# Decoder layer on one core: a second V buffer, five output places, and a table of places for each group of a batch

## What is computed

```python
x = x + _L0_attn_ref(_layernorm(x), wq, bq, wk, bk, wv, bv, wo, bo)   # q, k, v, softmax(q k^T) v, wo
x = x + _L0_xattn_ref(_layernorm(x), ctx_512, Wq, Wkv_expand, Wout)   # keys and values from the latent, causal
x = x + _L0_ffn_ref(_layernorm(x), proj1, proj1_bias, proj2, proj2_bias, gate_w)  # gelu(x p1 + b1) p2 + b2
```

## Time and profile before

| | us |
|---|---|
| median of 3 runs | 1224.34 (1221.7 to 1225.97) |
| the profiled execution | 1223.58 |
| its span, first to last instruction | 1221.8 |
| TensorE busy | 1162.2 (95%) |
| VectorE busy | 674.4 (55%) |
| ScalarE busy | 483.3 (40%) |
| GpSimd busy | 431.5 (35%) |

### The profile page before, as it was taken

The page is one execution under the profiler, slowest core; times in us unless marked ns, Lnnn a source line. Parts: engine busy times, 40 slices in busy tenths (PEclk is TensorE's granted clock), DMA queues, the critical chain, the costliest instruction groups (busy, mean ns, idle before and its releaser), DMA issues.

```text
span 1221.8 us, 15866 instructions
## 1 busy us (share of the span) xinstructions
PE 1162.2 (95%) x6016; PEld 774.1 (63%) x6016; DVE 674.4 (55%) x966; ACT 483.3 (40%) x792; POOL 431.5 (35%) x398
## 2 busy tenths in 40 slices
PE   5989999999999899999999999999999999999998
PEld 4645566466556544555656565655787887887886
DVE  5656757665776467567667567564454233233222
ACT  4345544545453556535445454554131111111110
POOL 1226632643444756534426347564101001001000
PEclk9979999999999999999999999999999999999999
DMA  6823322342143434514525436420320000000000
GB/s 234 265 87 116 110 77 74 107 122 86 55 119 104 138 109 125 151 62 141 164 86 150 118 104 190 122 69 1 95 87 1 35 1 1 34 0 0 35 1 35
DMA packets 73735, 110.30 MB, mean 90 GB/s; under 512 B 6976, under 2 KB 45888, under 8 KB 71744
## 3 DMA queue, kind: packets, MB, share of 16 engines
q1 hardware_dynamic: 70864, 102.00, 27.8%
q0 software_dynamic: 2080, 6.82, 2.0%
q10 hardware_dynamic: 720, 0.54, 0.1%
HBM read 71.58 MB, written 37.75 MB: 89 GB/s over the span
## 4 chain that ended last, share of the span: by engine, by line
PE 83%; DVE 8%; POOL 3%; ACT 3%; issue 2%; DMA 1%; SPq 0%; DVEq 0%; ACTq 0%; POOLq 0%
PE PS L865 17%; PE PS L866 16%; PE PS L867 16%; PE PS L997 12%; PE PS L982 9%; PE PS L960 8%; DVE m_cols L1203 5%; PE PS L992 2%; PE PS L985 1%; PE PS L963 1%; DVE xTL L1169 1%; ACT PT L784 1%; POOL P_sum L648 1%; POOL P_sum L654 1%; PE PS L879 1%
## 5 line engine op out<-in xcount | busy, mean ns | idle before, releaser
L1203 DVE TENSOR_REDUCE m_cols<-PS 128x1 f32<-128x512 f32 (+3 forms) x432 | 281.8, 668 | 170.2 <-PE PS L960 96.8
L784 ACT ACTIVATE PT<-PS 128x512 f32<-128x512 f32 (+1 forms) x432 | 240.4, 580 | 158.0 <-PE PS L982 69.0
L648 POOL TENSOR_TENSOR P_sum<-PT 128x512 f32<-128x512 f32 x128 | 161.4, 1281 | 355.0 <-ACT PT L784 354.9
L960 PE MATMUL PS<-stackK,stackQ 96*128 96x512 f32 (+3 forms) x512 | 188.3, 404 | 12.2 <-DVE m_cols L1203 10.3
L982 PE MATMUL PS<-stackQ,stackK 100*128 100x512 f32 (+3 forms) x512 | 181.9, 399 | 6.7 <-ACT PT L784 6.5
L837 ACT ACTIVATE hid<-PS,b1c 128x512 f32<-128x512 f32 x64 | 44.1, 690 | 280.2 <-PE PS L867 278.2
L1284 DVE CAST hidH<-hid 128x512 fp32r<-128x512 f32 x64 | 30.6, 478 | 225.0 <-ACT hid L837 222.9
L960 PEld LDWEIGHTS PS<-stackK,stackQ 96*128 96x128 f32 x512 | 92.4, 192 | 80.8 <-DVE m_cols L1203 45.0
L1211 DVE RECIPROCAL P_sum<-PS 128x512 f32<-128x512 f32 x32 | 107.5, 3358 | 56.3 <-PE PS L997 56.3
L982 PEld LDWEIGHTS PS<-stackQ,stackK 100*128 100x128 f32 x512 | 90.3, 190 | 67.5 <-ACT PT L784 30.3
L654 POOL TENSOR_TENSOR P_sum<-P_sum,PT 128x512 f32<-128x512 f32 x96 | 120.5, 1282 | 4.5
(11 more groups left out here) (112 smaller groups left out, 1685.9 us busy)
## 6 DMA issues: line engine op xcount, KB each, us to landing
scratch<-stage SPq DMA_DIRECT2D x128, 256.0 KB, 2.9
stackK<-scratch SPq DMA_DIRECT2D x62, 256.0 KB, 3.9
stackQ<-scratch SPq DMA_DIRECT2D x46, 256.0 KB, 3.7
stackQ<-scratch SPq DMA_DIRECT2D x18, 512.0 KB, 4.8
stackK<-scratch SPq DMA_DIRECT2D x60, 128.0 KB, 4.1
stackQ<-scratch SPq DMA_DIRECT2D x28, 128.0 KB, 3.6
PT<-wT SPq DMA_DIRECT2D x3, 1024.0 KB, 8.6
x_res<-x SPq DMA_DIRECT2D x3, 1024.0 KB, 9.1
```

What stands on the lines that cost most here:

```text
L648: pool.tensor_tensor(P_sum[:, h, :], PT[:, h, :], PT[:, 4 + h, :], ALU.add).then_inc(p_added, 1)
L784: nc.scalar.activation(PT[:, slot:slot + heads, q0:SEQ], PS[:, T_BANK + n % 2, 0:heads * width].rearrange("p (h n) -> p h n", h=heads), AC ...
L960: mm = nc.tensor.matmul(dst[:, a, :], stackQ[0:STACK, par, h + a, q * P:(q + 1) * P], stackK[0:STACK, par, h + a, 0:n], start=a == 0, stop ...
L1203: nc.vector.tensor_reduce(m_cols[:, q, STACK + h:STACK + h + heads], PS[:, S_BANK + m % 2, 0:heads * n].rearrange("p (h n) -> p h n", h=he ...
```

## The change

A buffer `V_odd` is added; V of odd batches lives there, V of even ones in `V`. The weight of V, staged in `V` at the start, is staged in `V_odd`. `oTH_more` and `oTL_more` are a fifth place for outputs: unit u uses place u % 5, and the copy of the output waits for Wo of the batch before one unit later (g = 1). `PLACES` becomes a table for each layer and each group, with a bend in the spread of maxima and of fill; `FILL` lists by group what is filled in and in which order. Of a self batch, Wo stands half in the first and half in the second unit, V half in the third and half in the fourth. In the cross layer the second unit has Wo 2 and 3 and V 1, the third V 0 and 2, the last V 3. Q no longer leads each unit. `PARTIAL` puts parts of the last output product into units 30 and 31 (before: 29, 30 and 31). The steps on raw weights get other places. The SBUF reserve for DMA descriptors is set to 4096 bytes a partition. What is awaited as the last V, Wo or xT is looked up (`last_of`), since tile 3 is no longer always the last.

```diff
-CHUNK_PLACES = [(25, (10.0, 12.0)), (26, (10.0, 12.0)), (28, (7.0, 10.0)), (28, (16.0, 20.0)), (29, (10.0, 12.0)),
-                (30, (10.0, 12.0))]
+RAW_PLACES = ((0.0, 1.69, 4.59, 10.14), (16.96, 21.63), (24.23,), (3.78, 24.23, 13.17, 13.33), (13.88,))
+CHUNK_PLACES = [(25, (9.05, 14.91)), (26, (12.2, 12.85)), (28, (7.02, 9.29)), (28, (11.79, 18.46)), (29, (9.87, 17.97)), (30, (12.51, 14.11))]
 PLACES = {
-    SELF: dict(body=(32.85, 16.28, 17.5, 28.5),
-         scores=((0.0, 0.6), (2.6, 0.7), (5.8, 0.91), (9.6, 0.8)),
-         values=((6.1, 6.2, 10.3, 14.0), (6.1, 6.2, 10.2, 13.7), (6.1, 6.2, 10.2, 13.7), (6.1, 6.2, 13.9, 14.0)),
-         max_first=4.46,
-         q=(0.2, 5.3),
-         k=(4.35, 10.48),
-         rest=8.66,
-         stats=0.5, divide=0.0,
-         output=3.49),
...
+    SELF: (dict(body=22.55,
+                scores=((0.0, 0.6), (2.33, 0.68), (5.8, 1.05), (9.38, 0.98)),
+                values=(5.7, 8.52, 11.43, 17.73),
+                maxima=(3.34, 12.22, 21.58),
+                fill=(0.0, 11.04, 23.33),
+                stats=2.01,
+                divide=-4.58,
+                output=4.27),
+           dict(body=26.97,
+                scores=((0.0, 0.56), (2.6, 0.78), (5.72, 0.91), (9.6, 0.68)),
+                values=(6.06, 6.55, 10.78, 13.55),
+                maxima=(4.46, 10.29, 24.38),
+                fill=(0.14, 10.85, 26.15),
+                stats=6.13,
+                divide=4.43,
+                output=5.43),
...
+FILL = {
+    SELF: (("K", "Q", ("Wo", 0), ("xT", 0), ("xT", 1), ("xT", 2), ("Wo", 1), ("xT", 3)),
+           (("Wo", 2), "K", ("Wo", 3), "Q"),
+           (("V", 0), "K", ("V", 3), "Q"),
+           (("V", 2), ("V", 1), "Q", "K")),
+    CROSS: (("K", "Q", ("Wo", 0), ("xT", 0), ("xT", 1), ("Wo", 1), ("xT", 2), ("xT", 3)),
+            ("K", ("Wo", 3), ("V", 1), ("Wo", 2), "Q"),
+            (("V", 0), ("V", 2), "K", "Q"),
+            ("K", "Q", ("V", 3))),
+}
+PARTIAL = ((30, 7.12, 0), (30, 8.89, 1), (31, 9.81, 2))
...
+def bent(items, first, middle, last):
+    half = len(items) // 2
+    return spread(items[:half], first, middle) + spread(items[half:], middle, last)
...
+    for use in FILL[layer_of(u)][g]:
+        if use in ("Q", "K"):
+            fill += [(use, u + 3, k) for k in range(pieces_of(use, u + 3) if u + 3 < UNITS else 0)]
+        elif use[0] == "xT":
+            fill += [(*use, 0)]
+        elif b if use[0] == "Wo" else b < LAST:
+            fill += [(*use, k) for k in range(GROUPS if use[0] == "Wo" else pieces_of("V", b + 1))]
+    work += bent(fill[:-TAIL], *places["fill"])
...
+        V_odd = sb("V_odd", [P, KT, DIM], F32)
+        oTH_more = sb("oTH_more", [P, SEQ], F32R)
+        oTL_more = sb("oTL_more", [P, SEQ], F32R)
...
+        def values_of(b):
+            return V_odd if b % 2 else V
+        def oH(u):
+            return oTH_more[:, :] if u % 5 == 4 else oTH[:, u % 5, :]
...
-                if g == 0 and b:
-                    act.wait_ge(g_full, FULL["Wo", b - 1, KT - 1] + 1)
-                nc.scalar.activation(oTH[:, g, :], oT[:, :], ACT.Copy).then_inc(oH_done, 1)
+                if g == 1 and b:
+                    act.wait_ge(g_full, FULL[last_of("Wo", b - 1)] + 1)
+                nc.scalar.activation(oH(u), oT[:, :], ACT.Copy).then_inc(oH_done, 1)
...
-                    nc.vector.tensor_tensor(V[:, t, :], G(name), bv_b, ALU.add).then_inc(g_done, 1)
+                    nc.vector.tensor_tensor(values_of(b)[:, t, :], G(name), bv_b, ALU.add).then_inc(g_done, 1)
...
-    nc = bacc.Bacc("TRN2", target_bir_lowering=False, num_devices=1)
+    nc = bacc.Bacc("TRN2", target_bir_lowering=False, num_devices=1, dynamic_dma_scratch_size=4096)
```

More of the change, by code:

```diff
@@ L174, in pe_order @@
         work.append((first + h * step, "scores", j, 0))
-    work += [(place, "values", k, 0) for k, place in enumerate(places["values"][g])]
+    work += [(place, "values", k, 0) for k, place in enumerate(places["values"])]
     if u + 1 < UNITS:
-        first, last = places["max_first"], body
+        first, middle, last = places["maxima"]
         sizes = [heads * (keys(u + 1, q) + P) for q, _, heads in S_FILLS[layer_of(u + 1)]]
         for j in range(len(sizes)):
-            work.append((first + (last - first) * sum(sizes[:j]) / sum(sizes[:-1]), "max", j, 0))
+            part = 2 * sum(sizes[:j]) / sum(sizes[:-1])
+            work.append((first + (middle - first) * min(part, 1) + (last - middle) * max(part - 1, 0), "max", j, 0))
         work.append((body + 1.0, "turn", u + 1, 0))
@@ L183, in pe_order @@
         work += spread([("up", i, k) for i in range(2) for k in range(KT)], 1.0, 13.0)
[L184 to L186 removed]
+    work += [(place + t, "partial", t, piece) for unit, place, piece in PARTIAL if unit == u for t in (0, 1)]
     work.append((body + 2.0, "sums", 0, 0))
     fill = []
[L189 to L191 removed]
@@ L215, in pe_order @@
+    kinds = [item[1] for item in work]
+    assert [kind for kind in kinds if kind in ("values", "sums")][-1] == "sums"
+    assert [item[2] for item in work if item[1] == "xT"] == (list(range(KT)) if g == 0 else [])
+    assert not any(item[1:3] == ("Wo", 0) for item in work) or g == 0
+    assert "xT" not in kinds or not {"Q", "K"} & set(kinds[kinds.index("xT"):])
     return work
@@ L311, with last_of @@
 USES, FULL, DONE, HIGHS = bank_uses()
+def last_of(what, b):
+    last = max(((what, b, t) for t in range(KT)), key=lambda name: FULL[name])
+    assert DONE[last] == max(DONE[what, b, t] for t in range(KT))
+    return last
 BANK = {name: GENERAL[n % 2] for n, name in enumerate(USES)}
```

132 lines of the change are left out of this document (77 added, 55 removed).

## The result

The changed kernel takes 1178.63 us in the median (1177.89 to 1179.48), the kernel before 1225.15 beside it; the ratio is 0.9625, with a 95% interval of 0.9605 to 0.9646.

A forecast was written before the change was run, and what follows sets the result against it. TensorE was taken as the bound, with hidden waits on VectorE's reads to win back. Gains of 9.2 + 8.9 + 1.4 + 4.7 + 2.7 + 7.8 + 3.6 = 38.3 us gave 1186 us, range 1168 to 1213.

The forecast's parts named there:

- under 6%: Sign, unit 5 of the changed kernel: VectorE's maxima (m_cols) hold under 6% of the chain of waits.
- the 4.6 a batch: Units 4 to 11: products moved into thin units cover waits on VectorE, 4.6 us a batch, 9.2 for two.
- even cover: Rival: a product hides as much wherever it stands; self batches give nothing, 1211 us; sign: units 5, 6 at 27.5; chance 0.24.
- its waits for the transposes stay: Unit 4: TensorE's waits at the transposes of the next x remain; the unit goes from 35.7 to 29.7 us.
- Unit 0: Normalization behind all 16 exponentials and most maxima out earlier remove a stall and slow clock: gain 8.9 us, to 25.7.
- Units 1 to 3: Batch 0 after unit 0: changes of -0.3, +2.1 and -0.4 us, together a gain of 1.4.
- Units 12 to 15: Unit 12 gains 4.7 us from fewer weight splits ahead and a later normalization; units 13 to 15 gain 2.7.
- Cross batches: Batches 4 to 6: products moved out of the first unit save its waits and cover others, 2.6 us a batch, 7.8 together.
- it will be VectorE that ends last: Unit 23: losing 3 products gains nothing, since VectorE's statistics come ahead of the maxima (16.97 busy of 19.9 us).
- The better tables: Rival: tables by group also thin each unit's first third, 0.8 us a unit, 25 us less, 1161 us; chance 0.12.
- The banks: Rival: the two banks all products share become the wait, 52 uses at 1.0 us, slower at 1238 us; chance 0.07.
- The clock: Rival: many short waits pull the clock down, once in each of 16 cross units, 26 us, 1212 us; chance 0.03.

The follow-up runs named there:

- experiments 8: The kernel before, with VectorE taking each maximum over 256 columns in place of 512: 1201.95 us, ratio 0.9823.
- experiment 9: The changed kernel, with VectorE taking each maximum over 256 columns in place of 512: 1174.71 us, ratio 0.9602.
- experiment 4: The changed kernel with old orders, but in units 4 to 11 output product and V moved and spread by the old rules: 1218.36 us, ratio 0.9957.
- Experiment 2: The changed kernel with every unit's order as before, except unit 0, which has its new order: 1214.77 us, ratio 0.9927.
- experiment 7: The kernel before, with ScalarE's first normalization in unit 0 put behind its 16 exponentials: 1221.88 us, ratio 0.9986.
- experiments 1: The changed kernel with all orders and raw-weight places as before; second V buffer, fifth output place and smaller DMA scratch stay: 1224.65 us, ratio 1.0004.
- 3: The changed kernel with every unit's order as before, except units 4 to 11, which have their new orders: 1213.55 us, ratio 0.991.
- 5: The kernel before, with VectorE's reciprocal of the sums replaced by a plain copy: 1222.81 us, ratio 1.0002.
- 10: The changed kernel with own tables for units 3, 7, 11, 14, 15, 29 and 30, products placed early: 1184.24 us, ratio 0.969.
- 11: The changed kernel with only the first fill item moved earlier in units 3, 7, 11, 14, 15, and unit 29's own table: 1180.97 us, ratio 0.9655.

## Why the prediction was right, and where it was off

**The bound, and what bunching costs: right.** Waits on VectorE's reads, hidden under TensorE's busy time, were what there was to gain (experiments 8 and 9, and the 18.9 us by which TensorE's busy time fell outside unit 0). The chain of unit 5 holds no m_cols, where under 6% had been asked for. The reason held more strongly than it was used: "one product between two score tiles is enough" is what the new order does and the mere move doesn't (experiment 4).

**Self batches: 11.3 for 9.2, and two steps mis-sized.** First, the 4.6 a batch was worked out from products alone, as though the count did it. By experiment 4 the count gives 2.2, and the places the other 3.6. Unit 5 with the move alone takes 27.3, which is close to the 27.5 that the prediction set as the mark of even cover; with the places, 26.1 and so below the 26.5 forecast. That the number came out near was in part luck, since two errors offset: too much for the move, nothing for the order inside the unit. Second, in unit 4 "its waits for the transposes stay" was wrong. The waits of TensorE in that unit on the read of a transposed x were 1.2 us:

```profile
PE PS L865 <- DVE xTL L1169: 1.2, 2, 0.7
```

The changed kernel's unit 4 has no such wait; other tiles stand between the transposes and the next output product. Unit 4 took 28.5 where 29.7 had been forecast, 1.2 less. The prediction had the order of `FILL` before it, but not the order with score tiles sorted in.

**Unit 0: 9.3 for 8.9.** 25.3 us at clock 1.00, against 25.7. Experiment 2 shows that the gain belongs to this unit's order, and experiment 7 that moving ScalarE's normalization, which the prediction put first, isn't enough by itself: TensorE's part of the order is needed too. Whether that is the later transposes or the maxima ahead of them, which the second half of its sentence named, is open.

**Units 1 to 3: 1.4 for 1.4, with luck.** The terms were -0.3, 2.1 and -0.4; the units gave 0, 2.2 and -0.8 (23.2, 26.5 and 26.8 us after). The misses cancel.

**Units 12 to 15: 6.3 for 7.4.** Unit 12 gave 40.9 - 5.56 - 29.2 = 6.1 for 4.7: its clock is 1.00, and GpSimd is off its path, as the chain by line shows beside the earlier trace rows. Of the 6.1, 1.2 are the clock alone (39.7 us at 1.00 in experiment 2). How the rest divides between GpSimd's steps and the normalization wasn't tried.

```profile
by line: PE PS L1084 21.4%; PE PS L1047 13.4%; PE PS L1069 12.7%; PE PS L951 11.4%; PE PS L952 11.2%; PE PS L953 11.1%; PE PS L965 5.8%; ACT PT L870 4.7%; issue 3.3%; ACT WH L849 2.5%; DVE x_res L1283 2.4%; PE PS L1079 1.5%; ACTq L867 0.1%;
```

Units 13 to 15 gave (435.1 to 502.2, 67.1 us) + 5.56 - 72.5 = 0.2 for 2.7; this is the one clear miss. By unit: 13 gave 0.9 of 1.9, 14 0.1 of 0.6, and 15 lost 0.8 where 0.2 had been forecast. The forecast had priced their products like those of units 5 to 7, and this is the step that failed. Units 14 and 15 keep few of them (the next batch's V is one piece a tile in the cross layer), yet follow tables made for 16. Their chains by line show what is bare then, maxima in unit 14, and in unit 15 GpSimd and ScalarE:

```profile
by line: PE PS L1084 26.5%; PE PS L1069 18.0%; PE PS L1047 16.9%; DVE m_cols L1290 14.7%; ACT PT L870 5.2%; PE PS L951 5.1%; PE PS L952 5.1%; PE PS L953 5.0%; PE PS L1079 2.8%; issue 2.2%; ACTq L867 0.2%
```

```profile
by line: PE PS L1084 17.8%; POOL P_sum L734 16.7%; PE PS L1069 11.3%; ACT PT L870 10.5%; PE PS L1047 7.9%; issue 7.9%; PE PS L951 6.0%; POOL oTL_more L724 5.5%; PE PS L952 5.0%; PE PS L953 5.0%; PE PS L1079 2.8%; DVE m_cols L1290 2.5%; PE P
```

Whether better places would mend it is open: both attempts made unit 14 longer, the second one (24.5 us) with a clock of 0.93 in that unit, which explains all of its 1.4. Unit 15's waits on GpSimd weren't tried. Such falls of the clock aren't the order's doing alone: unit 14 in its old order takes 23.1 to 23.2 us at 0.93 in the profiles of experiments 1, 3 and 5, and 21.8 to 21.9 at 1.00 in those of the kernel before and of experiments 2, 4 and 7.

**Cross batches: 10.9 for 7.8.** The first unit's own waits were 1.6 and I took 1.2 of them, plus 1.1 in the second; those terms were of the right kind. The failed step is "it will be VectorE that ends last" in unit 23. Its chain by line:

```profile
by line: PE PS L1084 20.8%; PE PS L1047 16.3%; PE PS L1069 15.7%; PE PS L951 10.0%; PE PS L953 7.8%; PE PS L952 7.7%; PE PS L1050 5.9%; PE PS L1072 5.1%; ACT stackQ L855 4.3%; ACT PT L870 3.3%; PE PS L1079 2.4%; issue 1.6%
```

No line of VectorE is in it. The unit takes 18.1 us, near 19.9 less its three products. It had been called a loss "for nothing" in words, while the sum took those 2.1 us off all the same: words and sum didn't agree, and the sum was right. What the units gave, by the borders (589.5, 621.9, 639.5, 657.0, 676.9 before; 556.7, 581.3, 604.5, 622.4, 640.5 after) and 0.695 us a product: 2.2 in the first, 0.7 in the second, 1.0 in the third, where 1.2, 1.1 and 0.3 had been forecast, and -0.3 in the last. The first unit's excess is again the waits for transposed x: 1.3 us before, none after.

**Units 28 to 31: 4.0 for 3.6. The start and the last part:** 1.8 us had not been forecast. The last part is 372.6 in experiment 1 too (852.4 to 1225.0), with the old order of attention, so that its 1.0 is no more than executions differ; for the 0.8 at the start nothing was tried.

**The rivals.** Even cover is ruled out by units 5 and 6 (26.1 and 26.6, not 27.5), but 27.3, close to it, is what the move without the places gives. The better tables, with a chance of 0.12, are half true: the places brought more than half of the self batches' gain. The banks: no wait of a V or output product on VectorE's read of an earlier one appears among TensorE's visible waits; those on a transposed x fell from 11.5 to 2.9. The clock: in the profiled execution it is 1.00 from unit 0 to the last part, with 24 waits of the score tiles for exponentials among it. The Trainium skill (TensorE: Matmul & The Clock Gate, A second HAM failure mode: psum-queue depth-cycling) describes a clock that swings between its levels where TensorE idles briefly between groups of matmuls frequently enough; this profile shows no such swing. It is one execution, though. The other three list a mean clock of 0.998 to 0.999, and in near relatives of the changed kernel one unit had a short fall: unit 15 in experiment 9 (24.1 us, clock 0.93), unit 13 in 10, unit 14 in 11. That price, some 1.1 to 1.7 us once in a kernel, is far from the 26 us of the rival. The kernel did what it says (experiments 1 to 3).

## What to carry to other kernels

Where a busy engine follows a slower reader over two buffers, price its waits by start-to-start spacing, and look at what stands between two uses of the buffers: one piece of other work in each gap is worth more than the same pieces in a block, and a few pieces moved to cover one wait uncover another. Before asking for less work on the engine that others wait for, test which of its operations anybody waits for: cutting 0.67 us reads to 0.41 gave 21.5 us, and dropping 85 us of reciprocals gave nothing. A price per product taken from full units doesn't carry over to units with less fill: units 13 to 15 gave 0.2 of 2.7 us. Whether tables of their own would give it isn't shown: of those tried, unit 29's gained 0.6 us, and the others gained 0.1 or lost time.
